# Row maxima of causal attention scores: taken by key tile in the layout of the scores, with VectorE's transposing maximum

## The reference, cut to what matters

```python
scores = jnp.einsum('bqhd,bkhd->bhqk', q_full, k_full) * softmax_scale   # S = 1024, H = 32
scores = jnp.where(causal[None, None], scores, jnp.finfo(scores.dtype).min)
attn = jax.nn.softmax(scores, axis=-1)
out = jnp.einsum('bhqk,bkhd->bqhd', attn, v)
```

## Time and profile before

| | |
|---|---|
| median of 3 runs | 752.55 us (752.33 to 752.96) |
| span of the profiled execution, first to last instruction | 751.0 us |
| PE busy in the span | 719.2 us (96%) |
| DVE busy | 541.3 us (72%) |
| ACT busy | 326.3 us (43%) |
| POOL busy | 207.5 us (28%) |
| granted clock of PE, mean | 0.999 of full |

### The profile page before, as it was taken

How to read it: one execution, slowest core, us unless ns; L and a number is a source line. 1 busy time by engine, 2 the same in 40 slices (tenths; PEclk the granted TensorE clock), 3 DMA queues, 4 the chain that set the end, 5 groups by cost and what they waited for, 6 DMA issues and landing times.

```text
span 751.0 us, 10449 instructions
## 1 busy us (share of the span) xinstructions
PE 719.2 (96%) x3829; PEld 502.7 (67%) x3829; DVE 541.3 (72%) x802; ACT 326.3 (43%) x499; POOL 207.5 (28%) x197
## 2 busy tenths in 40 slices
PE   2889999999999999999999999999999999999997
PEld 1756566666666666666666666555788888887886
DVE  6878689799799799799799889686893323213432
ACT  4844545545545545554554444444254322222210
POOL 1149534144144144144144020100463000000211
PEclk9999999999999999999999999999999999999999
DMA  8934633403403403403403580440210422200101
GB/s 319 257 84 111 142 76 85 103 1 85 103 0 85 103 1 85 103 1 84 104 2 83 123 327 2 168 168 1 84 29 1 127 84 63 58 10 1 42 30 43
DMA packets 40211, 63.43 MB, mean 84 GB/s; under 512 B 4512, under 2 KB 20896, under 8 KB 38304
## 3 DMA queue, kind: packets, MB, share of 16 engines
q1 hardware_dynamic: 40160, 62.75, 30.6%
HBM read 32.99 MB, written 2.10 MB: 47 GB/s over the span
## 4 chain that ended last, share of the span: by engine, by line
PE 72%; DVE 22%; issue 3%; ACT 1%; DMA 1%; SPq 0%; DVEq 0%; ACTq 0%
PE PS L987 16%; PE PS L811 8%; PE PS L1004 8%; PE PS L892 7%; PE PS L874 7%; PE PS L881 6%; PE PS L877 6%; DVE PR L1539 5%; PE PS L951 5%; DVE NMa L1449 4%; PE PS L802 4%; DVE wide L1539 3%; PE PS L824 2%; DVE NMd L1454 2%; DVE NMb L1449 1%
## 5 line engine op out<-in xcount | busy, mean ns | idle before, releaser
L1199 ACT ACTIVATE PR<-PS 128x1024 f32<-128x1024 f32 (+1 forms) x144 | 133.1, 929 | 149.1 <-PE PS L881 118.0
L811 PE MATMUL PS<-KH,Q 96*128 96x128 f32 (+3 forms) x576 | 131.2, 330 | 6.2 <-DVE NMa L1449 4.8
L1449 DVE TENSOR_REDUCE NMa<-PS 128x1 f32<-128x512 f32 (+3 forms) x184 | 117.7, 657 | 25.0 <-PE PS L811 22.8
L811 PEld LDWEIGHTS PS<-KH,Q 96*128 96x128 f32 x576 | 86.7, 190 | 60.9 <-issue 32.4
L874 PE MATMUL PS<-Q,KH 96*128 96x512 f32 x288 | 118.6, 412 | 0.0
L1539 DVE TENSOR_TENSOR PR<-PR 128x2048 f32<-128x2048 f32 (+3 forms) x56 | 112.8, 2014 | 3.6 <-ACT PR L1199 1.2
L881 PE MATMUL PS<-Q,KH 97*128 97x512 f32 (+1 forms) x288 | 114.2, 397 | 0.2 <-DMA Q<-NM 0.2
L877 PE MATMUL PS<-Q,KL 96*128 96x512 f32 (+1 forms) x288 | 113.6, 394 | 0.0
L1787 POOL TENSOR_SCALAR_AFFINE_SELECT diag<-diag 128x512 f32<-128x512 f32 x64 | 47.3, 739 | 195.9 <-ACT diag L1142 195.7
L874 PEld LDWEIGHTS PS<-Q,KH 96*128 96x128 f32 x288 | 54.6, 189 | 27.8 <-issue 14.3
L892 PE MATMUL PS<-PR,V 128*32 128x512 f32 (+3 forms) x704 | 70.2, 486 | 0.0
(11 more groups left out here) (192 smaller groups left out, 1066.9 us busy)
## 6 DMA issues: line engine op xcount, KB each, us to landing
Q<-TQ SPq DMA_DIRECT2D x56, 384.0 KB, 6.2
RT<-in_wo SPq DMA_DIRECT2D x4, 1024.0 KB, 4.8
TQ<-in_wo SPq DMA_DIRECT2D x4, 1024.0 KB, 5.1
Q<-TQ SPq DMA_DIRECT2D x16, 192.0 KB, 3.4
WI<-in_gate_w SPq DMA_DIRECT2D x10, 256.0 KB, 3.5
WI<-in_up_w SPq DMA_DIRECT2D x10, 256.0 KB, 3.9
DI<-in_down_w SPq DMA_DIRECT2D x10, 256.0 KB, 2.7
PR<-in_wmod_c SPq DMA_DIRECT2D x2, 1024.0 KB, 6.5
```

The costliest lines, as they stand in the source:

```text
L811: ins = pe.matmul(bank[:, i * w:(i + 1) * w], M.Q[0:KR, g % 2, 0, qt // 4, h0 + i, qs], M.KH[0:KR, lo:lo + w], start=(i == 0), stop=(i == ...
L1199: act.activation(tiles, banks, ACT.Exp).then_inc(S_.p, 1)
L1449: dve.tensor_reduce(dst, PS[:, bank_of(turn), 0:n * w].rearrange("p (h k) -> p h k", k=w), axis=AX.X, op=ALU.max, negate=True).then_inc(S_ ...
```

## The change

A part becomes one matmul with the layout of the scores: 128 keys on the partitions, 4 heads x 128 queries along the free side, one for each pair of query tile and key tile, 36 for a group, diagonals among them. DVE's maximum with `apply_transpose=True` turns 32 x 32 blocks on its way and so takes the maximum over 32 keys at a time, into `MX`. `join` then takes the maximum over the key tiles with two reductions, PE transposes 128 x 128, and DVE (no longer ACT) takes the maximum of the last four numbers from PSUM (`rows_reduced`). ACT and POOL have no part in it any more: the diagonal blocks are masked by the idle contraction rows, as in the exact scores. For that all 31 mask rows are now used in the high product as well (`mask_rows`, `mask_levels`), so the parts wait for the mask rows, whose copy for odd groups is split in two DMAs, one of them issued earlier. The maxima go out from 128 partitions with 32 numbers each instead of 32 with 128. The parts' order becomes query tile by query tile, and the table spaces all of them evenly at 0.7 us.

```diff
-PARTS = maxima_parts()
+PARTS = [(qt, kt) for qt in range(NS) for kt in range(qt + 1)]
...
     def maxima_part(g, k):
-        qt, lo, w, h0, n = PARTS[k]
+        qt, kt = PARTS[k]
+        f, rows = qt // 4, P if is_diagonal(k) else KR
         bank = side_bank(TURN[("part", g, k)])
-        qs = slice(qt % 4 * P, qt % 4 * P + P)
-        for i in range(n):
-            pe.wait_ge(S_.q[qt // 4][h0 + i], 16 * (g + 1))
-            ins = pe.matmul(bank[:, i * w:(i + 1) * w], M.Q[0:KR, g % 2, 0, qt // 4, h0 + i, qs],
-                            M.KH[0:KR, lo:lo + w], start=(i == 0), stop=(i == n - 1))
-        ins.then_inc(S_.side, 1)
+        if kt == 0 and qt % 4 == 0:
+            for h in range(HG):
+                pe.wait_ge(S_.q[f][h], 16 * (g + 1))
...
+        pe.matmul(bank, M.KH[0:rows, kt * P:(kt + 1) * P], M.Q[0:rows, g % 2, 0, f, :, qt % 4 * P:(qt % 4 + 1) * P],
+                  start=True, stop=True).then_inc(S_.side, 1)
...
-        dve.tensor_reduce(dst, PS[:, bank_of(turn), 0:n * w].rearrange("p (h k) -> p h k", k=w), axis=AX.X, op=ALU.max,
-                          negate=True).then_inc(S_.free[bank_of(turn) - FIRST_BANK], 1)
-
-    def diagonal_reduced(g, qt):
...
+        dve.tensor_reduce(M.MX[:, kt, qt // 4, :, qt % 4, :],
+                          PS[:, bank_of(turn), :].rearrange("p (h s q) -> p h s q", h=HG, q=L), axis=AX.X, op=ALU.max,
+                          apply_transpose=True).then_inc(S_.free[bank_of(turn) - FIRST_BANK], 1)
...
-        dve.tensor_tensor(M.NMj[:], M.NMa[:], M.NMd[:], ALU.min).then_inc(S_.nm, 1)
+        for f in range(2):
+            dve.tensor_reduce(M.NMj[:, f].rearrange("p h n s -> p (h n s)"),
+                              M.MX[:, 0:NS // 2 * (f + 1), f].rearrange("p k h n s -> p (h n s) k"), axis=AX.X,
+                              op=ALU.max).then_inc(S_.nm, 1)
+
+    def rows_reduced(g):
...
+        dve.tensor_reduce(M.NM[:], PS[:, bank_of(turn), 0:P].rearrange("p (k q) -> p q k", q=L), axis=AX.X, op=ALU.max,
+                          negate=True).then_inc(S_.free[bank_of(turn) - FIRST_BANK], 1)
...
-    cost = [0.35 if is_diagonal(k) else 0.14 + PARTS[k][2] * PARTS[k][4] / 960 for k in range(len(PARTS))]
...
+    places = [(begin + (end - begin) * k / len(PARTS), ("part", k), 0.7) for k in range(len(PARTS))]
+    return places + [(end + 0.02, ("join",), 1.2), (end + 0.12, ("rows",), 0.3)]
```

More of the change, by code:

```diff
@@ L88, in mask_rows @@
     for n, (start, size) in enumerate(mask_levels()):
-        hide, keep = (30, 45) if size == 2 else (20, 32)
-        row = (n // MASK_ROWS, 1 + n % MASK_ROWS)
+        hide, keep, near = (20, 32, 4) if size == 4 else (16, 23, 0)
+        row, at = 1 + n, 0
         for i in range(size):
-            q[row + (start + i,)] = -2.0 ** (hide - i * (hide + keep))
-            k[row + (start + 1 + i,)] = 2.0 ** (i * (hide + keep))
-        k[row + (slice(start + size + 1, P),)] = 2.0 ** ((size - 1) * (hide + keep))
+            if i > 0:
+                at += hide + (keep if i % 2 == 0 else near)
+            q[0, row, start + i] = -2.0 ** (hide - at)
+            if i % 2 == 0:
+                q[1, row, start + i] = -2.0 ** (hide - at)
+            else:
+                k[0, row, start + 1 + i:] = 2.0 ** at
+            k[1, row, start + 1 + i:] = 2.0 ** at
     k[1, 0] = 1.0
@@ L395 @@
 SLACK = 0.04
-LEAST_BEHIND = 3
 def maxima_places(begin, end):
-    cost = [0.35 if is_diagonal(k) else 0.14 + PARTS[k][2] * PARTS[k][4] / 960 for k in range(len(PARTS))]
-    diagonals = [k for k in range(len(PARTS)) if is_diagonal(k)]
-    at = lambda k: begin + (end - begin) * sum(cost[:k]) / sum(cost)
-    places = []
-    for k in range(len(PARTS)):
-        for qt, d in enumerate(diagonals):
-            if k == min(d + LEAST_BEHIND + 1, (diagonals + [len(PARTS)] * 2)[qt + 2]):
-                places.append((at(k), ("least", qt), 0.65))
-        places.append((at(k), ("part", k), 0.0 if is_diagonal(k) else cost[k]))
-    return places + [(end + 0.02, ("join",), 0.1), (end + 0.12, ("rows",), 0.3)]
+    places = [(begin + (end - begin) * k / len(PARTS), ("part", k), 0.7) for k in range(len(PARTS))]
+    return places + [(end + 0.02, ("join",), 1.2), (end + 0.12, ("rows",), 0.3)]
 def group_places(g, places):
@@ L670, in sp_program @@
         if w == 0:
-            sp.wait_ge(S_.pj, NS)
             sp.wait_ge(S_.nd, 16)
-            for hl in range(2):
-                copy_mask_rows(hl, S_.mq)
+            copy_mask_rows(1)
         if w < G - 2:
@@ L872, in scores @@
             if w == 1:
-                pe.wait_ge(S_.mq, 32)
+                for hl in range(2):
+                    pe.wait_ge(S_.mq[hl], 16)
         pe.matmul(dst, M.KH[0:KR, ks], M.Q[0:KR, w % 2, 0, qb, :, qs], start=True, stop=False)
@@ L1121, in latent_high @@
         act.activation(M.TQ[:, 2, 0, cols], PS[:, bank_of(turn), :], ACT.Copy).then_inc(S_.lh, 1)
-    def rows_copied(g):
-        turn = TURN[("rows", g)]
-        act.wait_ge(S_.side, turn + 1)
-        if g > 0:
-            act.wait_ge(S_.nd, 16 * g)
-        act.activation(M.NM[:], PS[0:HG * NS, bank_of(turn), 0:P], ACT.Copy).then_inc(S_.free[bank_of(turn) - FIRST_BANK], 1)
     def gate_copied(key):
@@ L1163, in side @@
             gate_copied(key)
-        elif key[0] == "rows":
-            rows_copied(key[1])
         elif key[0] == "split":
             split_high(key[1], key[2])
-        elif key[0] == "part" and is_diagonal(key[2]):
-            diagonal_copied(key[1], key[2])
         elif key[0] == "high":
@@ L1511, in side @@
             latent(g, key[2])
-        elif kind == "part" and not is_diagonal(key[2]):
+        elif kind == "part":
             part_reduced(g, key[2])
-        elif kind == "least":
-            diagonal_reduced(g, key[2])
+        elif kind == "rows":
+            rows_reduced(g)
         elif kind == "join":
@@ L1780, in rotated_sum @@
         pool.tensor_tensor(M.RT[:, 3, :], M.RT[:, 2, :], M.RT[:, 3, :], ALU.add).then_inc(S_.re, 1)
-    def diagonal(g, k):
-        qt = PARTS[k][0]
-        tile = M.diag[:, qt % 2]
-        pool.wait_ge(S_.free[bank_of(TURN[("part", g, k)]) - FIRST_BANK], freed(("part", g, k)))
-        pool.affine_select(out=tile, in_=tile, compare_op=ALU.is_ge, fill=MASKED, base=0, pattern=[[0, HG], [-1, P]],
-                           channel_multiplier=1).then_inc(S_.ds, 1)
     def split_low(g, hf):
@@ L1806, in side @@
             weights_low(g)
-        elif kind == "part" and is_diagonal(key[2]):
-            diagonal(g, key[2])
         elif kind == "even" and g in HANDED:
```

107 lines of the change are left out of this document (40 added, 67 removed).

## The result

The changed kernel takes 760.4 us, the median of 4 runs (759.85 to 761.03), against 752.52 (752.33 to 752.96) for the kernel before beside it: a ratio of 1.0103, with a 95% interval from 1.0089 to 1.0117. It is 1% slower; 756.4 was forecast. The profiled execution took 759.9 us with a span of 758.1, against a span of 751.0 before, and the granted clock is 1.0.

What follows compares the result with a forecast made beforehand. PE and DVE were both taken as near their limit, with the maxima's delivery ending windows 1 to 5. First stage -2.0, window 0 0, windows 1 to 5 +7.0, window 6 -1.2 gave +3.8: 756.4 us, range 748.5 to 763.5.

Steps and rivals of the forecast that it cites:

- DVE's part: DVE's reductions and join for a group: 24.2 us, 2.1 more than before, with a transposing pitch of 0.64.
- T: The end of step 7's addition in a full window, at 243.65 in the profile before.
- the side remark on it: Hopping reads of `MX` might add about 0.5 us to each `join`, 3 to 4 us in all.
- Up to step 7's addition: Full window's start to that addition's end: about 0.1 us earlier, bounds 1.3 earlier to 0.5 later.
- From there to the next window: Behind step 7's addition: reductions, join, step 8's addition, last maximum, DMA; maxima landed 9.0 us later, 1.5 later than before.
- The delivery decides: At a full window's end the maxima's DMA, landed at T + 9.0, sets the time; PE is ready at about T + 8.2.
- Window 0: 0: Window 0 has no denominators near its start, so PE keeps some 1.4 us up to T: no change.
- Window 6: -1.2: Window 6 has no queries and PE leads: half of PE's 2.4 us gain, 1.2 us shorter.
- First stage: -2.0: Stage before window 0: reductions and join end at 80.0 instead of 82.3, the stage 2.0 us earlier on 85.58.
- Rival A: PE keeps its gain as the windows' bank waits dissolve, T 2.0 us earlier: -8.0, 744.5 us; chance 0.22.
- Rival B: DVE's transposition is free, pitch 0.60: +1.0 in all, 753.6 us, no change; chance 0.18.
- Rival C: DVE's reductions don't overlap (0.72) and the join takes 1.4: 765 us; chance 0.12.

Runs made afterwards that it cites:

- e_contig: Changed kernel with `MX` laid out key tile last, so the join reads neighbours: 755.5 us, ratio 1.0041.
- e_const: Changed kernel sending a constant tile of -60 instead of the negated maxima for groups 1 to 7, without waiting for the last maximum: 754.1 us, ratio 1.0021.
- e_ports: Changed kernel with two POOL pieces moved in windows 0 to 5, a normalisation to unit 18 and the queries' low part to unit 28: 755.1 us, ratio 1.0037.
- e_keep1: Changed kernel with one idle product instead of two behind every second part of the first stage: 758.6 us, one run.
- e_all: Changed kernel with the edits of e_contig, e_keep1 and e_ports together: 750.7 us, ratio 0.9969.
- late against early instruction: Changed kernel with one idle DVE maximum more in each of windows 0 to 6: 769.0 us in unit 28 (late), 760.5 in unit 5 (early).
- the parts at 0.60: Changed kernel with a group's parts spread over 0.03 to 0.60 of a window instead of 0.76: 761.2 us; with the maxima's transposition also in unit 32: 762.7.
- both orders: Changed kernel with parts spread to 0.60 of a window, the maxima's transposition beside the join (761.2 us) or in unit 32 (762.7 us).

## Why the prediction was right, and where it was not

Direction and main place were right. Of the difference, 7.79 us lie in windows 1 to 5, where +7.0 was forecast, and the wait for the maxima's DMA stands in the profile where it was named. By its steps:

- **DVE's part.** The pitch of the transposing maximum was put at 0.64 and is 0.604; the join at 0.93 and is 1.53; the last maximum at 0.28 and is 0.29. The first two errors half cancel behind T: -0.29 and +0.60. The join lies outside its own bounds (0.36 to 1.4): the price left out that the source hops, and only the side remark on it had the size. e_contig shows it: 0.60 a group come back.
- **Up to step 7's addition.** Forecast 0.1 earlier against the window's start, measured 0.48 (48.22 instead of 48.70), inside its bounds. That addition takes 3.04 and not 2.71, as POOL's low part now ends 0.90 into it and before ended 0.55 into it. "They stay" was said of POOL's work beside the additions; its instructions stay, their overlap does not.
- **From there to the next window.** Forecast T + 9.0 against 7.55 before, measured T + 9.40; the join brings most of it, and the DMA lands 2.3 us behind its issue, not 2.2. "The delivery decides" holds: without it the window ends 0.94 earlier (e_const), where the text had put PE 0.8 before the delivery. Under it lies a second chain, addition 8 to its exponential, that keeps 0.62 us of the loss.
- **Window 0: 0** was wrong, +0.82 measured. It ends by the same chain: e_const takes 0.70 from it and e_ports 0.64.
- **Window 6: -1.2** was right, -1.34 measured.
- **First stage: -2.0** is the step that failed, -0.17 measured. 0.6 of the 1.8 is the join, and 0.35 that the queries' last DMA lets PE go at 61.65 and not at 61.3. The rest is the sentence "the matmuls on constants there still fit": they don't, 21 reductions took 13.8 us (66.76 to 80.55) where 21 pitches of 0.604 are 12.7, and with half of these products gone the stage is 0.87 shorter (e_keep1, e_all).
- **Sum.** +3.8 forecast, +7.1 measured in the spans: the first stage 1.8, window 0 0.8, windows 1 to 5 0.8, less 0.1 in window 6, make the 3.3 missed. The other 0.7 us between 756.4 and 760.4 lie between the runs' median and the profiled span, 2.3 us and not 1.55. Every execution whose span is known took 1.8 us more than its span (here 759.92 and 758.1); the 1.55 set a median of several against the span of one, and the median after lies 0.5 above the profiled one.

Rival A (PE keeps its gain) was not met: T moved up by 0.48, and it needed more than 0.85. Rival B's price (pitch 0.60) came true and its time (753.6) did not, as the join took back more than that gave. Rival C's pitch is refuted, its join (1.4) was nearest to the measured 1.53.

What is shown: the chain behind step 7's addition (late against early instruction), the join's hop (e_contig), the delivery (e_const), the wait for POOL (e_ports). Read from the traces alone: that the lower clock, and not the new order, took the gain of the parts at 0.60. Open: why the same pause of PE is followed by a fall in one window and not in the next, and what the parts at 0.60 would give with `split` kept where e_ports has it, which was not run.

## What to carry to other kernels

Price work by its place: the same 1.1 us instruction cost 0 us or 8.6 us a run (1.1 a window, and a lower clock in some), and an engine's pause is slack only if nobody who ends it has waited for that engine before. When an edit moves a planner's places, read every engine's new neighbours, those of the unchanged work too; here a transposition beside its join (2 us a window) and a GpSimd piece beside the last addition (1.5 us) each made PE pause. Before an order is given up for its time, compare windows of equal clock: in the one window at the full clock that each profile holds, both orders were 1.5 us faster than the kernel after (their window 0 was 2.5 and 2.7 us slower), and the clock hid it. Lay out an intermediate for its reader: writes 8 numbers apart by the transposing maximum cost nothing here, reads that hop cost 0.6 us a group.
